# Adapted two-layer kernel on one core: the down adapter's first factor is prepared behind the next part's first gate tile and the last activation

## What is computed

```python
# layer 1: mixing by a chosen 64x64 matrix, then an effective linear map
x = x + ffn0(cond0(x, weights[itok_B_0_15]))
# layer 2, its first half (F = 2752, rank 16, one of 16 adapters a batch)
gate = x @ W_gate.T + 0.5 * adapter(x, A_gate, B_gate)
up   = x @ W_up.T   + 0.5 * adapter(x, A_up, B_up)
act  = silu(gate) * up
down = act @ W_down.T + 0.5 * adapter(act, A_down, B_down)
# layer 2, its second half
x = x + down @ sign(weight).T + bias
```

## Time and profile before

| | us |
|---|---|
| median of 3 runs | 1939.13 (1939.07 to 1940.69) |
| the profiled execution, its own time | 1940.12 |
| its span in the profile | 1938.4 |
| TensorE (PE) busy | 1912.4 (99%) |
| VectorE (DVE) busy | 1472.0 (76%) |
| ScalarE (ACT) busy | 765.0 (39%) |
| GpSimd (POOL) busy | 542.1 (28%) |

### The profile page before, as it was taken

The page is one execution under the profiler, slowest core; times in us unless marked ns, Lnnn a source line. Parts: engine busy times, 40 slices in busy tenths (PEclk is TensorE's granted clock), DMA queues, the critical chain, the costliest instruction groups (busy, mean ns, idle before and its releaser), DMA issues.

```text
span 1938.4 us, 31452 instructions
## 1 busy us (share of the span) xinstructions
PE 1912.4 (99%) x9104; PEld 1607.2 (83%) x9104; DVE 1472.0 (76%) x2459; ACT 765.0 (39%) x1441; POOL 542.1 (28%) x935
## 2 busy tenths in 40 slices
PE   7999999999999999999999999999999999999998
PEld 6878888888988888888898888888889888888887
DVE  5877877778677777877777877777877787777786
ACT  4353333333344333433444434343335443334331
POOL 4542222212415122221422422212061322222100
PEclk9999999999999999999999999999999999999999
DMA  8755445543466554444447655454344655555411
GB/s 233 164 114 112 100 105 121 117 98 80 128 142 130 109 108 101 101 100 94 125 108 143 125 116 109 106 114 100 68 114 123 139 121 111 121 110 113 99 44 44
DMA packets 320629, 218.38 MB, mean 113 GB/s; under 512 B 177192, under 2 KB 311208, under 8 KB 320544
## 3 DMA queue, kind: packets, MB, share of 16 engines
q1 hardware_dynamic: 281952, 188.43, 42.8%
q0 software_dynamic: 36352, 24.19, 6.9%
q10 hardware_dynamic: 2240, 4.72, 0.7%
HBM read 204.35 MB, written 12.58 MB: 112 GB/s over the span
## 4 chain that ended last, share of the span: by engine, by line
PE 90%; DVE 4%; ACT 3%; issue 2%; DMA 0%; SPq 0%; DVEq 0%; ACTq 0%
PE ps L1492 25%; PE ps L1494 25%; PE ps L1493 25%; PE ps L1703 6%; PE ps L1630 2%; DVE ps L935 2%; PE ps L1550 2%; PE ps L1551 2%; PE ps L1515 1%; DVE split L921 1%; PE ps L1569 1%; PE ps L1516 1%; DMA nat<-x 0%; ACT split L632 0%; ACT hidden L632 0%
## 5 line engine op out<-in xcount | busy, mean ns | idle before, releaser
L1492 PE MATMUL ps<-x,split 128*128 128x512 f32 x1376 | 538.8, 392 | 2.1 <-DVE split L921 1.5
L1494 PE MATMUL ps<-x,split 128*128 128x512 f32 x1376 | 536.8, 390 | 0.0
L1493 PE MATMUL ps<-x,split 128*128 128x512 f32 x1376 | 536.0, 390 | 0.0
L632 ACT ACTIVATE split<-ps 128x512 fp32r<-128x512 f32 x344 | 203.1, 599 | 450.9 <-DVE ps L935 441.7
L531 POOL DMA_DIRECT2D nat_ad<-L_cond_A_down x224 | 137.0, 618 | 735.1 <-DVE ps L935 725.8
L1494 PEld LDWEIGHTS ps<-x,split 128*128 128x128 f32 x1376 | 258.7, 188 | 56.1
L1493 PEld LDWEIGHTS ps<-x,split 128*128 128x128 f32 x1376 | 258.8, 188 | 54.8
L1492 PEld LDWEIGHTS ps<-x,split 128*128 128x128 f32 x1376 | 259.3, 188 | 51.7 <-DVE split L921 3.1
L1492 PE MATMUL ps<-hidden 128*128 128x512 f32 x672 | 261.5, 389 | 0.0
L1493 PE MATMUL ps<-hidden 128*128 128x512 f32 x672 | 261.5, 389 | 0.0
L1494 PE MATMUL ps<-hidden 128*128 128x512 f32 x672 | 261.4, 389 | 0.0
(11 more groups left out here) (141 smaller groups left out, 2760.2 us busy)
## 6 DMA issues: line engine op xcount, KB each, us to landing
nat<-L_cond_W_gate SPq DMA_DIRECT2D x336, 128.0 KB
nat<-L_cond_W_up SPq DMA_DIRECT2D x336, 128.0 KB
nat_down<-L_cond_W_down SPq DMA_DIRECT2D x112, 384.0 KB, 6.4
nat_a<-L_ffn_weight SPq DMA_DIRECT2D x128, 128.0 KB, 2.7
nat<-effective_weight SPq DMA_DIRECT2D x24, 512.0 KB
nat<-x SPq DMA_DIRECT2D x16, 512.0 KB
nat_b<-L_cond_B_gate POOLq DMA_DIRECT2D x224, 24.0 KB, 2.2
nat_b<-L_cond_B_up POOLq DMA_DIRECT2D x224, 24.0 KB, 2.1
```

The source lines that it names most:

```text
L632: act.activation(dst, src, func).then_inc(piece_hi, 1)
L1492: pe.matmul(dst, a[0], b[0], start=first, stop=False)
L1493: pe.matmul(dst, a[0], b[1], start=False, stop=False)
L1494: return pe.matmul(dst, a[1], b[0], start=False, stop=last)
```

## The change

In the parts that are not the last of a group, the piece AD goes behind nextG0 in the list of pieces, and behind nextG0 and act_tile 2 in the orders of ScalarE and VectorE. TensorE's wait for its words goes from the head of `down_part` to just ahead of the rank products. In the last part AD keeps its place, under the name "lastAD"; `PART[:12]` leaves the list as long as it was. GpSimd's wait for AD goes by the name, and so follows the piece.

```diff
-PART = (["U1"] * 2 + ["D0"] * 2 + ["G2"] * 2 + ["D1"] * 2 + ["U2"] * 2 + ["D2"] * 2 + ["AD"] + ["nextG0"] * 2
+PART = (["U1"] * 2 + ["D0"] * 2 + ["G2"] * 2 + ["D1"] * 2 + ["U2"] * 2 + ["D2"] * 2 + ["nextG0"] * 2 + ["AD"]
         + ["Sq"] * 2 + ["nextB"] * 3 + ["nextU0"] * 2 + ["nextG1"] * 2)
-LAST = PART[:13] + ["S6"] * 2 + ["BD"] * 2 + ["DREM"] * 2 + ["S7"] * 2
+LAST = PART[:12] + ["lastAD"] + ["S6"] * 2 + ["BD"] * 2 + ["DREM"] * 2 + ["S7"] * 2
@@ ScalarE
+            def a_down_tiles(g, q, name):
+                c = first_of(name, g)
+                piece(g, q, c, lora_ad[:, :, 0::3, :],
+                      bank_of(c)[:, 0:PT * P].rearrange("p (j h r) -> p j h r", j=PT, h=2))
+
             def part(g, q, last):
@@ ScalarE, part
                 down_tile(g, q, 2)
-                c = first_of("AD", g)
-                piece(g, q, c, lora_ad[:, :, 0::3, :],
-                      bank_of(c)[:, 0:PT * P].rearrange("p (j h r) -> p j h r", j=PT, h=2))
                 if last:
+                    a_down_tiles(g, q, "lastAD")
...
                 unit(g, q, "nextG0", SPLIT_GU + 6)
                 act_tile(g, q, 2)
+                a_down_tiles(g, q, "AD")
                 sign_unit(g, q, "Sq", q)
@@ VectorE
-            def a_down_tiles(g, q):
-                c = first_of("AD", g)
+            def a_down_tiles(g, q, name):
+                c = first_of(name, g)
@@ VectorE, part
                 down_tile(g, q, 2)
-                a_down_tiles(g, q)
                 if last:
+                    a_down_tiles(g, q, "lastAD")
                     sign_part(g, q, "S6", 6)
...
                 weight_unit(g, q, "nextG0", NAT_GU + 6, SPLIT_GU + 6)
                 act_tile(g, q, 2)
+                a_down_tiles(g, q, "AD")
                 sign_part(g, q, "Sq", q)
@@ TensorE, down_part
-                pe.wait_ge(piece_lo, START + low_number(g, q, first_of("AD", g) + 1))
+                def wait_factors(name):
+                    pe.wait_ge(piece_lo, START + low_number(g, q, first_of(name, g) + 1))
...
                     for i in range(3, KC):
                         bank_read(i)
                         tiles(i, range(PT)).then_inc(down_psum, 1)
+                    wait_factors("AD")
                     for half in range(2):
                         bank_read(KC + half)
                         ranks(half, range(PT), True).then_inc(down_psum, 1)
                     return
+                wait_factors("lastAD")
                 for half in range(2):
                     ranks(half, (0, 1), False)
```

## The result

The changed kernel takes 1958.69 us (median of 5 runs, 1957.89 to 1961.3), the kernel before 1939.49 us in the same comparison: a ratio of 1.0097 (95% interval 1.0086 to 1.0108), 1% slower. The profiled execution has a span of 1957.0 us, where it was 1938.4.

A forecast was written before the change was run, and what follows sets the result against it. TensorE, busy 99% of the span, was taken as the bound. Gain -2.5 us plus stalls +19.9 us made +17.4 us on the median 1939.13, so 1956.5 us; range 1945.3 to 1964.0.

The forecast's parts named there:

- The gain at nextG0: TensorE's four waits for split words at part 0's nextG0, one per group, go: 0.79 + 3 x 0.56 = 2.5 us won.
- rival C: Another wait replaces TensorE's at part 0's nextG0, so the 2.5 us gain is missing: 1959.0 us, chance 0.03.
- Nothing won before act_tile 2: In looping parts VectorE's wait for TensorE before act_tile 2 grows from 2.57 to 4.29 us; the multiply starts as before.
- The chain of nextB moves along: Behind act_tile 2, VectorE's sign turn and all that follows, up to nextB's last low words, come 1.72 us later.
- The stall: The late first down add frees PSUM bank 3 late; TensorE stalls 0.83 us at the fourth down tile, 24 times: +19.9 us.
- GpSimd and SyncE at no cost: Their shifted loads, including GpSimd's of nat_ad and nat_b, delay nothing in the looping parts.
- TensorE's moved wait at no cost: The wait for AD words, moved ahead of the rank products, comes some 15 us after they are made: nothing.
- Rival A: First add's delay stays hidden if under about 0.8 us, leaving only the gain: 1936.6 us, 0.13% faster, chance 0.07.
- Rival B: TensorE's clock falls to 1.2 GHz at the new stalls in each of 24 parts: 2026 us, chance 0.04.
- Rival B's price: One clock fall at 104 to 110 us lost 2.9 us over 16 matmul steps; 24 such would be 70 us.
- The start of the kernel: Up to group 0's part 0 ranks: 0.83 us of new stall less 0.79 us of wait removed at nextG0.

The follow-up runs named there:

- experiment 2: Experiment 1 with VectorE doing the AD tile behind the first three down adds instead of ahead of the first: 1936.77 us, ratio 0.9985 to the kernel before.
- experiment 3: Changed kernel with the fourth down tile in PSUM bank 1 instead of 3, plus a wait in the next part's U0: 1937.65 us, ratio 0.9984 to the kernel before.
- experiment 4: Kernel before, nothing moved; VectorE repeats a half-tile subtraction four times behind the last activation tile in parts 0 to 5: 1963.57 us, ratio 1.0122.
- experiment 5: Kernel before, nothing moved; one extra half-tile subtraction on VectorE behind the last activation tile in parts 0 to 5: 1941.11 us, ratio 1.0001.
- experiment 6: Kernel before with only the bank change: fourth down tile in PSUM bank 1, plus a wait in the next part's U0: 1940.29 us, ratio 0.9996.
- experiment 7: Kernel before with only TensorE's wait for the AD words moved to just ahead of the rank products: 1940.41 us, ratio 1.0.
- experiment 1: Changed kernel with the AD piece moved behind nextB, directly ahead of the first down add: 1959.69 us, ratio 1.0104 to the kernel before.

## Why the prediction was right

It said 1956.5 us, +17.4; the measured medians differ by 19.2 and the spans by 18.6. The mechanism is the one that was forecast: the four waits at nextG0 go, and 24 waits at bank 3 come. Both terms were too small, the gain by 0.9 us and the loss by 2.8, so a part of the closeness is luck: the two errors work against each other.

- **The gain at nextG0** was forecast as 2.5 us, "all that can be won". The four waits are gone, so rival C did not come, and the gain is 3.4 us. It can be read without the stall in experiments 2 and 3. In the three later groups it is as forecast: from the first rank product of the last part to that of the next group's part 0 it is 176.05 to 176.08 us in the kernel before and 175.47 to 175.50 in these two, 0.57 to 0.61 us less (0.56 forecast). In group 0 it is 1.6 us where 0.79 was forecast: from the matmul behind TensorE's wait of 2.8 us for `lora_b_rem`, which lies ahead of all that was changed, to the first rank product it is 161.19 - 104.48 = 56.71 us before, and 158.93 - 103.83 = 55.10 and 158.74 - 103.68 = 55.06 in experiments 2 and 3. The forecast took the wait from one execution, and there it was short. Experiments 4 to 7 leave the AD tile at its place, and their waits at this point are 1.36 to 1.39 us, not 0.53. This is experiment 7:

```profile
104.42 0.53 PE L1550 MATMUL ps<-lora_t,lora_b_rem 128*128 128x256 f32 x2 [2.75 <-DVE lora_b_rem L921]
...
139.23 0.50 PE L1492 MATMUL ps<-x,split 128*128 128x512 f32 x1 [1.39 <-DVE split L921]
```

  At nextG0 TensorE goes on 34.79 to 34.81 us behind the matmul at `lora_b_rem` in all five profiles with the tile in its old place, when VectorE's words are there. But in the profile of before, where the granted clock was 0.50 until about 110 us, TensorE's own last matmul of U2 is 33.88 us behind it, and in the eight others 33.01 to 33.06. So it waited that much less there. By their ratios experiments 2 and 3 are 2.9 and 3.1 us faster than the kernel before, each with an interval of some 1.7 us to either side, which fits either size of the gain.
- **Nothing won before act_tile 2**: forecast 4.29 us of waiting, measured 4.30.
- **The chain of nextB moves along**: forecast 1.72 us for the whole of it; the last low words start 10.44 us behind the multiply (788.74 - 778.30) where it was 8.71 (781.91 - 773.20), 1.73 more.
- **The stall** was forecast as 0.83 us in 24 parts, 19.9 us. It is 0.85 to 1.01 in the looping ones (19.1 us) and, against experiments 2 and 3, 0.85 to 0.92 in the four parts 0 (3.6 us): 22.7 us. Two small terms were missed. The add does not overlap the low words of nextB by 0.09 us, but begins 789.62 - 789.60 = 0.02 us behind their end, 0.11 later than taken, which makes 0.94. And after the restart some matmuls step at 0.24 us instead of 0.227, which brings the part to 1.01. In group 0 it is less, see the last section. The sum is so 22.7 - 3.4 = +19.3 us.
- **GpSimd and SyncE at no cost**: in experiment 3 their loads go in the changed kernel's order, and TensorE has no wait from it. Experiment 1 moves the GpSimd load further (11.1 us behind the multiply) and 2 further still (13.6), with no effect of it. TensorE's moved wait at no cost: experiment 7.
- **Rival A** (the stall stays hidden) put its point of decision at 0.8 us of delay. 0.46 us leave no trace (experiment 5), and 1.72 and 1.84 us stall every part (1 and 4). Nothing was tried between them, so the point itself is bracketed and not measured. An estimate comes from the looping parts of groups 1 to 3: the changed kernel has 1.73 us of delay and 0.98 to 1.01 of stall, experiment 4 has 1.84 and 1.10 to 1.11 (its parts take 54.34 to 54.35 us), so 0.72 to 0.75 us are absorbed in both. In group 0 it is 0.88 to 0.89.
- **Rival B** (the clock falls) did not come: a pause of about 1 us every 54 us leaves TensorE at 2.4 GHz, as the row of 787 to 791 shows; over 600 to 960 us the granted clock is 1.00 too. The Trainium skill's warning of micro-pauses from cycling through PSUM banks (page "TensorE: Matmul & The Clock Gate", section "A second HAM failure mode: psum-queue depth-cycling") fits the pauses here, but this trace doesn't agree on the clock: no fall goes with them.
- **Rival B's price** was 2.9 us a fall, the time that TensorE's matmuls took longer at 104 to 110 us. But there the fall cost the kernel nothing. The way from `lora_b_rem` to the ranks is 56.69 to 56.72 us in the profile of before and those of experiments 5, 6 and 7, though the clock is back at 1.00 between 107 and 110 us in these three and only behind 110 us in the first. It is 55.98 us in the changed kernel, whose clock stays at 1.00, and 55.93 us in experiment 1, whose clock falls. What TensorE loses it would have spent waiting for VectorE. "One such fall" was not complete either: in the same trace the granted clock is 0.50 from 30 to 32 us, behind a wait of 2.13 us. In the changed kernel's profile it is 1.00 behind the same two waits, so whether it falls there differs from one execution to the next.
- **The start of the kernel** came out 1.49 us earlier, where +0.04 (0.83 - 0.79) was forecast. The matmul at `lora_b_rem` is at 104.48 before and 103.72 after; this 0.76 us is ahead of all that was changed, and in the nine profiles the place lies anywhere from 103.66 to 105.24. It is a matter of the single execution, and luck of this pair of profiles: without it the spans would differ by 19.4 us. The other 0.73 us are the change's own, 1.6 us won at nextG0 less 0.9 lost in part 0.

## What to carry to other kernels

Slack belongs to a place and not to an engine: VectorE idles a quarter of the time, yet had only 0.7 to 0.9 us to spare between the last activation and the first add, and a tile of 1.7 us put there made the fully busy TensorE wait in every part. Before moving work behind something, look for the next point in that queue which frees a buffer for the bound engine, and compare its slack with the whole length of what is moved, hand-overs to the other engine included. Behind that point (experiment 2), or with one more buffer (experiment 3), the same move is a small gain. And a wait that is read in one execution can be short because the waiting engine itself was late there: read it in more than one.

## What the runs showed that was not expected

The looping parts of group 0 stall less (0.85 us) than those of the other groups (0.98 to 1.01), with the same instructions. From the start of the adapter's last matmul in U2 to VectorE's multiply, which waits for it, it is 191.36 - 190.92 = 0.44 us in group 0 and 778.30 - 777.71 = 0.59 us in group 1 of the changed kernel:

```profile
190.92 0.40 PE L1556 MATMUL ps<-lora_t,lora_b 128*128 128x512 f32 x1
```

```profile
191.36 0.69 DVE L1161 TENSOR_TENSOR act_f<-ps,gated 128x512 f32<-128x512 f32 x1 [4.29 <-PE ps L1556]
```

The kernel before has the same difference further down: the first add waits 0.73 us in a looping part of group 0, 0.58 us in those of group 1:

```profile
203.16 1.96 DVE L1173 TENSOR_TENSOR acc<-ps,acc 128x512 f32<-128x512 f32 x3 [0.73 <-PE ps L1494]
```

The groups are written out one after the other, each with a loop of its own, so the same source line is other code in each. Why a hand-over takes 0.15 us more in one than in another was not tried and stays open. It bears on slack of this size: read it in every copy of a loop, and not in one.
